# Tiles 30 and 31 as a block pair, tile 30 converted on GpSimd, and the first slice mixed with zero-padded weights

## What is computed

```python
def cond(x, y, weight, mask, bias):           # y: 2x8, weight: 8x512x512
    masked_w = weight * mask[None, :, :]
    w_bot = jnp.einsum('bg,got->bot', y, masked_w)     # one 512x512 matrix for each batch
    return jnp.einsum('bnt,bot->bno', x, w_bot) + bias # x: 2x2048x512

def bitlinear(x, w):   # activations rounded to 255 steps of their row's largest, weights to -1, 0, 1 times their mean
    return jnp.einsum('bsi,oi->bso', act_quant(x), weight_quant(w))

h = cond(x, cond_8, weight, mask, bias)
out = x + bitlinear(silu(bitlinear(h, w_gate)) * bitlinear(h, w_up), w_down)   # inner width 2048
```

## Time and profile before

| | |
|---|---|
| median of 3 runs | 440.59 us (439.86 to 440.75) |
| the profiled execution | 440.59 us, its span 438.8 us, so 1.79 us lie around the span |
| PE matmul busy | 425.5 us, 97% of the span |
| DVE busy | 363.5 us, 83% |
| ACT busy | 336.8 us, 77% |
| POOL busy | 205.3 us, 47% |

### The profile page before, as it was taken

How to read it: one execution, slowest core, us unless ns; L and a number is a source line. 1 busy time by engine, 2 the same in 40 slices (tenths; PEclk the granted TensorE clock), 3 DMA queues, 4 the chain that set the end, 5 groups by cost and what they waited for, 6 DMA issues and landing times.

```text
span 438.8 us, 7668 instructions
## 1 busy us (share of the span) xinstructions
PE 425.5 (97%) x2318; PEld 257.5 (59%) x2318; DVE 363.5 (83%) x611; ACT 336.8 (77%) x474; POOL 205.3 (47%) x221
## 2 busy tenths in 40 slices
PE   4899999999999999999999999999999999999997
PEld 0234688888744455556555565655566555556555
DVE  0327768898897988899999999899999999899992
ACT  1215988778867976888888888888888888888871
POOL 0006999999149995142432423344142333414132
PEclk9999999999999999999999999999999999999999
DMA  7999999995142337254453635535263553535375
GB/s 277 404 396 408 308 335 339 313 251 144 36 98 48 61 66 187 48 145 85 134 120 73 146 70 143 97 118 120 76 157 64 135 115 100 120 87 142 80 162 154
DMA packets 104458, 69.79 MB, mean 159 GB/s; under 512 B 87280, under 2 KB 87536, under 8 KB 102896
## 3 DMA queue, kind: packets, MB, share of 16 engines
q1 hardware_dynamic: 103712, 67.13, 56.9%
q10 hardware_dynamic: 720, 2.36, 1.5%
HBM read 40.11 MB, written 8.39 MB: 111 GB/s over the span
## 4 chain that ended last, share of the span: by engine, by line
PE 59%; DMA 14%; issue 11%; DVE 9%; ACT 5%; POOL 1%; DVEq 0%; ACTq 0%; SPq 0%; POOLq 0%
PE ps L1308 15%; DMA wc<-wc 12%; PE ps L1171 11%; PE ps L1236 10%; PE ps L1126 8%; PE ps L1206 8%; PE ps L1164 4%; ACT wc L640 3%; DVE wc L954 3%; DVE wc L988 2%; DMA wc<-wcond 2%; PE ps L1139 2%; DVE p_part L1006 1%; ACT result L660 1%; PE ps L1243 1%
## 5 line engine op out<-in xcount | busy, mean ns | idle before, releaser
L1171 PE MATMUL ps<-tern_up,qT 128*128 128x512 f16 x512 | 131.1, 379 | 0.0
L1171 PEld LDWEIGHTS ps<-tern_up,qT 128*128 (+1 forms) x512 | 50.0, 98 | 54.5 <-DVE wc L988 0.4
L1006 DVE TENSOR_REDUCE p_part<-wc 128x1 f32<-128x1536 f32 x64 | 77.9, 1217 | 1.7
L988 DVE TENSOR_TENSOR wc<-ps,xT_sb 128x512 f32<-128x512 f32 x104 | 71.1, 683 | 7.3 <-issue 3.3
L640 ACT ACTIVATE wc<-wc 128x1024 f16<-128x1024 f32 x63 | 66.0, 1051 | 4.1 <-DMA wc<-wc 2.1
L623 ACT ACTIVATE wc<-wc,p_scale 128x2048 f32<-128x2048 f32 x30 | 60.1, 2002 | 4.3 <-DVE p_scale L1053 4.3
L1236 PE MATMUL ps<-wc 128*128 128x256 f16 x480 | 62.2, 273 | 0.7 <-DVE wc L954 0.7
L954 DVE TENSOR_TENSOR wc<-wc 128x1024 f16<-128x1024 f16 x60 | 56.9, 949 | 4.5 <-DMA wc<-wc 3.6
L1236 PEld LDWEIGHTS ps<-wc 128*128 128x128 f16 x480 | 46.9, 98 | 18.6 <-issue 1.2
L455 POOL TENSOR_SCALAR out_unit<-p_max,up_step,w_mean 128x1 f32<-128x1 f32 x32 | 11.3, 355 | 99.2 <-DVE p_max L1048 99.2
L618 ACT ACTIVATE xT_sb<-ps,gate_unit 128x512 f32<-128x512 f32 x78 | 49.2, 683 | 10.9 <-PE ps L1206 10.4
(11 more groups left out here) (142 smaller groups left out, 778.3 us busy)
## 6 DMA issues: line engine op xcount, KB each, us to landing
xT_sb<-xT SPq DMA_DIRECT2D x32, 256.0 KB, 6.6
x_res<-x SPq DMA_DIRECT2D x30, 256.0 KB, 2.9
out<-result SPq DMA_DIRECT2D x29, 256.0 KB, 2.4
wc<-wcond SPq DMA_DIRECT2D x12, 512.0 KB, 13.4
wc<-w_gate SPq DMA_DIRECT2D x4, 1024.0 KB, 16.0
wc<-w_up SPq DMA_DIRECT2D x4, 1024.0 KB, 8.4
wc<-w_down SPq DMA_DIRECT2D x4, 1024.0 KB, 6.1
wc<-wcond ACTq DMA_DIRECT2D x4, 512.0 KB, 7.7
```

Source lines behind the costliest of these rows:

```text
L988: nc.vector.tensor_tensor(prod[:, par, 512 * i:512 * i + 512], ps[:, UP + i % 2], source, ALU.mult).then_inc(prod_ready, 1)
L1006: nc.vector.tensor_reduce(p_part[:, par, i:i + 1], prod[:, par, 512 * lo:512 * hi], AX.X, ALU.max, apply_absolute_value=True).then_inc(par ...
L1171: ins = nc.tensor.matmul(ps[:, UP + i % 2], tile_of(s, k), tern_up[:, i, k], start=(k == 0), stop=(k == KH - 1))
```

## The change

Three edits.

1. The first slice. `mix_first` replaces `mix_products(0)`. A new tile `mix_pad` holds the mixing weights with zeros on either side, so that a matmul puts one batch's 16 rows into the upper or the lower half and zeros into the other; two matmuls accumulate in PSUM to a finished 32-row block of one batch. There are four matmuls for each chunk, sixteen for the slice, chunk after chunk: batch 0 to bank MIX, batch 1 to bank MIX + 1. DVE multiplies batch 0 by its mask straight out of PSUM (`mask_first`), ACT copies batch 1 once. Slices 1 to 3 are as before.

2. Tiles 30 and 31 become pair 15 (`LAST_PAIR`), in the same bank pair as the down products of step 3 use. Its seven block products stand in seven of the eight slots; `LATE_SLICES` goes. POOL makes its four input sums after those of pair 14. On ACT, `seed_bias` and `copy_first` for it are put between the rounding of tiles 29 and 28, `scale_down(3)` and `pair_convert(14)` go behind silu of step 0, both roundings follow in step 2, the two conversions at the ends of steps 3 and 4, and in step 2 the rounding of tile 1 is put ahead of the second silu. On DVE, `ternary_piece(2, 3)` moves behind step 0's `p_scale`. On SP the first two loads of `x_res` move behind the transposes of tile 1, the transposes of tiles 30 and 31 two steps later.

3. The end. POOL converts both halves of tile 30. ACT's last silu block comes behind the rounding.

```diff
-LATE_SLICES = {(0, 1): (0, 0), (0, 2): (0, 1), (0, 3): (0, 2), (1, 0): (0, 3), (1, 1): (1, 0), (1, 2): (1, 1),
-               (1, 3): (1, 2), (2, 0): (1, 3)}
+LAST_PAIR_SLOTS = {(0, 1): 0, (0, 2): 1, (0, 3): 2, (1, 0): 3, (1, 1): 4, (1, 2): 5, (1, 3): 6}
...
             for t in range(TILES):
...
                     if t == TILES - 1:
-                        convert_first_half(LATE)
+                        convert_half(LATE, 0)
+                        convert_half(LATE, 1)
...
                 if g is not None:
                     for i in (2, 3):
                         for q in range(2):
-                            silu_block(g, q, i)
+                            if not (s == TILES - 1 and i == 3 and q == 1):
+                                silu_block(g, q, i)
...
+                if s == TILES - 1:
+                    round_half(s - 1, 0)
...
+                    if s == 2:
+                        round_tile(s - 1, 1)
                     silu_chunk(s, 1)
...
                 if s == 0:
-                    pair_round(PAIR_END - 1, 1)
                     pair_round(PAIR_END - 1, 0)
-                    pair_convert(PAIR_END - 1)
+                    copy_first(LAST_PAIR)
...
+                if s == 0:
+                    scale_down(3)
+                    pair_convert(PAIR_END - 1)
                 if s == 2:
-                    cond_round(LATE + 1)
+                    pair_round(LAST_PAIR, 1)
+                    pair_round(LAST_PAIR, 0)
...
+            def mask_first():
+                dve.wait_ge(mix_psum, 1)
+                dve.wait_ge(s_mask[0][0], 16)
+                nc.vector.tensor_tensor(w_bot[:, 0, 0], ps[:, MIX], mask_sb[:, 0, 0], ALU.mult).then_inc(w_bot0_ready, 1)
...
+                if isinstance(s, int) and s == 1:
+                    pair_seed(LAST_PAIR)
                 product(s, par, 0, g)
...
                 if isinstance(s, int) and s == 0:
+                    pair_share(LAST_PAIR)
                     ternary_piece(2, 2)
-                if late is not None:
-                    cond_tile(late)
+                if isinstance(s, int) and s == 2:
+                    pair_largest(LAST_PAIR)
...
-                if isinstance(s, int) and s == 0:
-                    ternary_piece(2, 3)
+                if isinstance(s, int) and s == 1:
+                    pair_c22(LAST_PAIR)
...
+                if isinstance(s, int) and s == 0:
+                    ternary_piece(2, 3)
...
+            def mix_first():
+                for c in range(4):
+                    pe.wait_ge(s_wc[0][c], 16)
+                    for b in range(BATCH):
+                        for half in range(2):
+                            cut = T16 * ((1, 0), (2, 3))[b][half]
+                            ins = nc.tensor.matmul(ps[32 * c:32 * c + 32, MIX + b], mix_pad[:, cut:cut + 32],
+                                                   wc[:, 0, 2 * c + half], start=(half == 0), stop=(half == 1))
+                        if c == 3:
+                            ins.then_inc(mix_psum, 1)
...
+                if first and i == 0:
+                    pe.wait_ge(h_rounded, TILES)
...
-                    if (s, c) in LATE_SLICES:
-                        i, k = LATE_SLICES[s, c]
...
-                        cond_products(t, [k])
+                    if (s, c) in LAST_PAIR_SLOTS:
+                        pair_product(LAST_PAIR, LAST_PAIR_SLOTS[s, c])
```

More of the change, by code:

```diff
@@ L761, in _ @@
             act.wait_ge(half_ready, 1)
-            for k in range(KH):
+            act.wait_ge(mix_psum, 2)
+            nc.scalar.activation(w_bot[:, 1, 0], ps[:, MIX + 1], ACT.Copy).then_inc(half_copied, 2)
+            for k in range(1, KH):
                 act.wait_ge(mix_psum, 2 * k + 1)
@@ L1062, in _ @@
             mix_weights()
-            for k in range(KH):
+            mask_first()
+            for k in range(1, KH):
                 merge_halves(k)
```

103 lines of the change are left out of this document (58 added, 45 removed).

## The result

| | median | all executions | around the span |
| --- | --- | --- | --- |
| before | 440.48 us | 439.86 to 440.88 (6) | 1.8 us |
| after | 443.82 us | 441.50 to 446.28 (6) | 2.2 to 2.3 us, once 3.5 |

The ratio is 1.008, with a 95% interval of 1.006 to 1.010: slower by 3.3 us, where 440.0 was forecast and the range ended at 442.3. The profiled execution of after is the fastest of its six: 441.5 us, a span of 439.3 and 2.2 around it. So its trace shows only 0.5 us more in the span than before; the spans of the other five are 441.3 to 442.9 us, and of those there is no trace. All executions of this document are fast ones, and a ratio can differ a little from the quotient of the two medians.

A forecast was written before the change was run, and what follows sets the result against it. The prediction took PE to bound the kernel. Span 438.8 + 0.0 (opening) - 0.70 (pair) + 0.1 (end) = 438.2 us, with 1.79 around it 440.0; range 438.9 to 442.3.

The forecast's parts named there:

- Behind it PE is the bound, so -0.70 is kept: After step 4's down product (162.14 us before): the 0.70 us gained by then lasts to the end.
- nothing in between has slack to absorb it: Between two early places and the end: a shift of PE's work is carried through almost whole.
- Part 1, 0.0: Opening, first slice's mixing: products start at 15.6 us again, eight records behind the last chunk's landing; no gain or loss.
- the other case: Opening, a blocked load holding up all behind it: 26 records, +1.1 to +3.9 us, +2.9 taken as its value.
- how many pending instructions may be passed: Opening, PE's queue: left open by the trace of slice 1's mixing, which showed some ten passed.
- about as many here: Opening, PE's queue: the first slice needs about the some ten pending instructions passed in slice 1's mixing.
- column groups aren't independent: Opening: chunk 1's first weight load waits for chunk 0's last; 442.9 us (441.0 to 443.8), chance 0.12.
- chunks 2.6 us or more apart: Opening: chunk spacing that would show the ordering case, a blocked load holding up later chunks, to hold.
- Part 2, -0.70: Pair, steps 0 to 4: seven products for eight save PE 0.86 us; DVE lets 0.70 be kept.
- both covers: POOL's sums 4.0 us later: tile 0's unit and the first input sum still in time, by 0.4 and 0.8 us.
- Part 3, +0.1: End: tile 30's idle time moves to tile 31, gain 0; POOL's second conversion lengthens DVE's sum, 0 to +0.7 us.
- Around the span, 1.79 kept: Outside the traced span: the 1.79 us around it was added unchanged to the forecast span of 438.2.

The follow-up runs named there:

- f1: The whole change with 180 more idle waits on PE's sequencer: 440.89 us, ratio 1.000 to 1.003 to the kernel before.
- a1: The changed kernel run again, unaltered: 443.97 us, ratio 1.008 to 1.011 to the kernel before.
- d1: The kernel before with 73 more idle waits on PE's sequencer and nothing else changed: 443.14 us, ratio 1.004 to 1.007.
- d2: The kernel before with 217 more idle waits on PE's sequencer and nothing else changed: 439.98 us, ratio 0.999 to 1.001.
- a2: The changed kernel with the first slice mixed as before: 441.91 us, ratio 1.002 to 1.006 to the kernel before.
- c3: The kernel before with the pair alone, SP issuing tile 31's condition transpose and the last x loads later: 441.49 us, ratio 1.001 to 1.005.
- c4: The pair alone with SP's later transpose and loads, and GpSimd's pair 15 sums held until the first 16 tiles' units: 441.60 us, ratio 1.002 to 1.004.
- a3: The kernel before with only the new mixing of the first slice: 441.72 us, ratio 1.002 to 1.005.
- f2: The kernel before with only the new mixing, and 195 more idle waits on PE: 441.35 us, ratio 1.002 to 1.004.
- f4: The whole change with 34 unread matmuls ahead of the first mixing and 112 more idle waits on PE: 441.12 us, ratio 1.001 to 1.003.
- d4: The kernel before with the pair alone (old mixing, old end), and 192 more idle waits on PE: 439.93 us, ratio 0.999 to 1.001.
- g2: The pair alone with 192 more idle waits on PE, repeated in more rounds: 440.46 us, ratio 0.999 to 1.003 to the kernel before.
- c1: The kernel before with tiles 30 and 31 as a block pair alone (old mixing, old end): 441.02 us, ratio 1.002 to 1.005.
- c2: The kernel before with the new end alone: 440.29 us, ratio 0.9996 to 1.0016.
- g1: The pair alone with 34 unread matmuls ahead of the first mixing and 125 more idle waits on PE: 441.15 us, ratio 1.001 to 1.003.
- d3: The whole change with 104 more idle waits on PE's sequencer: 443.87 us, ratio 1.006 to 1.011 to the kernel before.

## Why the prediction was wrong

**The step that failed is "Behind it PE is the bound, so -0.70 is kept" (part 2).** The prediction costed instructions of five engines and SP's DMAs, and put what PE's own instruction packets do to other DMAs at nothing, without a reason. Added and removed instructions of PE move these packets, and in the profile of the changed kernel one of them fell into the transposes of tile 4. With the packets where they lay before, the change loses 0.6 us (f1), otherwise 3.3, and 4.0 in a1: 2.7 to 3.4 us go with their place. The step holds only as long as the transposes land 3.1 us after their conversion; a sum that is held up by 1.0 us begins with GpSimd's addition, not ahead of it, and lasts 1.8 us. The changed kernel's own profiles show 0.9 (after) and 1.9 us (a1) of such waits; that the executions of 444 us and more have further ones is inferred from f1, d1 and d2, not seen.

**What bounds the kernel.** PE, yes; but "nothing in between has slack to absorb it" is wrong for the profile that it was read from. From 16.3 to 118 us PE took back 1.2 us. In the kernel before PE's starts lie 0.2 us too far apart at 90.9, 97.2 and 103.5 and less at other places, 1.4 us in all from 56 to 110; after has 0.4. The ends of matmuls are modelled, so that such gaps stand as busy time in the earlier trace rows. They don't belong to the old kernel as such: d2, the same work with 217 idle instructions, has 0.4 too. From the first product to the first gate product it takes 98.45 us, the profile of before 99.47; a2, c3 and c4 take 99.4 to 99.8 as well, all other profiles 98.3 to 98.8. What makes the difference is open.

**Part 1, 0.0.** The first product came 0.71 us later in after's profile, 1.6 later in those of a3, f1 and f2, 0.1 earlier in f4. The groups are independent, as read from the earlier trace rows, but a chunk begins only with the fifth record of the one before: 4 + 4 + 4 + 8 = 20 records instead of the 8 behind the last landing. At the higher level (0.43 each) they would take 8.6 us from 5.6, to 14.2; then the landing of the last chunk (12.07 in the earlier trace rows) and eight records behind it set the end, as forecast, and in f4 they do. Each start at the lower level (0.85) adds 0.4, which the prediction allowed for in the other case only. The question it left ("how many pending instructions may be passed") was the right one, and its "about as many here" the wrong answer. The Trainium skill (TensorE: Matmul & The Clock Gate, "Part 3: Packing small matmuls — row/col tiling") has weight loads pulled ahead within a window of 64 when they go to another row group or to the background buffer. These go to other column groups, and here a handful was the limit. Its strict order of matmuls doesn't hold in this trace, with chunks 2.0 and 1.75 us apart where eight records take 3.4. In time the mixing costs 1.1 us (f2, 0.7 to 1.6), 0.2 of it around the span; in its profile 0.8 is the wait at 384 us. The whole change with the same mixing costs 0.6 (0.1 to 1.3), so the two just overlap.

The rival "column groups aren't independent" gave 442.9, near the result, for a reason that didn't occur: its mark, chunks 2.6 us or more apart, was met once (3.4) and missed twice.

**Part 2, -0.70.** The mechanism was right: the first down product came at 150.53, against "near 150.7", with 0.54 us idle next to DVE, and both covers held (169.90 without a wait). Of the 0.91, though, 0.48 is the middle's; the pair's own is 0.43, of the missing 0.27 us 0.17 because `add_blocks` took 1.57 instead of 1.40. Over the whole kernel it is worth nothing that can be measured: d4 and g2, the same program, came out 0.3 below and 0.2 above the kernel before. Part of it goes in 0.13 more around the span (c1, d4).

**Part 3, +0.1.** The profile gives +0.49. The term of the sum that was mis-sized is the lengthening of DVE's sum: 1.47 us, not 0.99 plus 0.1. The Trainium skill's rule (SBUF — State Buffer, "Who interferes with whom"), set aside for a milder row, was the better guide, for here too the sum grew by 0.48 and not by 0.1; and 1.83 for the sum at 190.49 is GpSimd's 1.27 and then some 0.6 of its own. In time the end cost 0.0 (-0.2 to +0.7), which admits both 0.1 and 0.5. The wait for tile 30 in the earlier trace rows was itself a packet's work: one comes at 422.9 in the kernel before, and both halves land 4.2 us after their conversion.

**Around the span, 1.79 kept.** It was 2.25: 0.2 with the mixing (a3, f2), 0.13 with the pair (c1, d4), 0 with the end (c2), and none with up to 217 more waits on PE (d1, d2: 1.81). With mixing and pair together it is 0.1 more than these make. What it is, no trace shows, since it lies outside them.

## What to carry to other kernels

Where a DMA's landing is nearly critical, compare the queues of instruction packets before and after an edit; a difference of one or two microseconds may belong to their place and not to the edit. To judge an edit, or before keeping or dropping one, run it with several numbers of idle instructions more on the bound engine (here 73 to 217): in this case the changed kernel took 440.9 or 443.9 and the kernel before 440.0 or 443.1, for the same work. And a forecast that rests on a wait going away should say what lies beside each instruction that comes in its place, GpSimd's additions of 512 columns above all.

## What the hardware showed

- PE's instructions come by DMA while the kernel runs, 16,384 bytes for about 256 records, 0.9 to 1.8 us on one DMA engine; none between about 235 and 390 us, in PE's loop. The Trainium skill (Trainium Architecture — The Big Picture, "The software stack") gives instructions of 64 bytes, which agrees, but has the streams moved into each engine's instruction memory when the program is loaded; on that the traces disagree with that section.
- A transposing DMA that meets such a packet lands up to 1.9 us late (5.0 us after the conversion instead of 3.1, f1), or, for 28 of 92, not late at all. Where one of 8,192 bytes was met instead, 47 of 125 landed 0.3 to 0.7 us late.
- A DVE addition of two SBUF tiles (0.69 us) that begins with a GpSimd addition of 1.27 us takes 1.8. Where it began 0.2 us behind one of 0.67 us and 0.4 ahead of the next, it took 0.99, and that next one 1.12 instead of 0.67 (f1 at 190.4 and 190.8).
- The granted clock rose to its higher level between 9.3 and 13.6 us in kernels whose PE does nothing before the first chunk (at 5.4 to 5.8 us), differently in each profile, whether PE then pauses between the chunks (before, 11.2) or not (after, 9.6; f1, 11.2); and at 5.6 (f4) and 7.3 us (g1) with PE busy from 1.5 us on.
- Near the end of d3, behind 2.00 us without a matmul, it was at its lower level again for 3.4 us.
